# Reordering the pieces of a pipelined ViT block on four engines

## The reference, cut to what matters

```python
h = layernorm(layernorm(patches(x)) @ W + b)         # 768 -> 192 (tok)
h = h + attn(ln(h))        # 12 heads of 16, causal, with a relative term, then a projection
n = ln(ln(h))              # the routed block
s = sigmoid(n @ Wr + br);  idx = top_k(-s, 29)       # 29 of 196 tokens
attn_out = softmax(q k / 4) v @ Wo + bo              # kept for the 29 tokens only
mix_out  = (n + s * pooled) @ Wm + bm                # for all the others
h3 = h + where(selected, attn_out, mix_out)
out = h3 + gelu(ln(h3) @ W1 + b1) @ W2 + b2          # 192 -> 768 -> 192
```

## Time and profile before

| what | value |
|---|---|
| median of 3 runs | 4944.79 us |
| the profiled execution's own time | 4944.02 us |
| its span in the profile | 4942.2 us |
| TensorE busy, matmuls | 4696.2 us (95%) |
| VectorE busy | 3872.3 us (78%) |
| ScalarE busy | 3448.9 us (70%) |
| GpSimd busy | 3065.9 us (62%) |
| granted TensorE clock, mean | 0.989 of full |

### The profile page before, as it was taken

One profiled execution on the slowest core, in us unless ns is written; L12 is line 12 of the kernel. 1 busy time (PEld: TensorE's weight loads), 2 busy tenths in 40 slices (PEclk: granted clock), 3 DMA queues, 4 the chain that ended last, 5 costly groups with the idle time before them and its releaser, 6 DMA issues. The chain is left out here.

```text
span 4942.2 us, 143405 instructions
## 1 busy us (share of the span) xinstructions
PE 4696.2 (95%) x44376; PEld 4299.3 (87%) x44376; DVE 3872.3 (78%) x13015; ACT 3448.9 (70%) x12030; POOL 3065.9 (62%) x4143
## 2 busy tenths in 40 slices
PE   3899999999999999999999999999999999999998
PEld 3788888888888888888888888888888888888887
DVE  3787887887888788788788878878878877887885
ACT  1667777776776777777677677777777767767775
POOL 2566666666666666666666666666666666666664
PEclk7899999999999999999999999999999999999999
DMA  5555555455555555555555555555554555555551
GB/s 70 68 68 72 69 71 72 66 74 67 69 73 67 72 70 70 72 67 73 69 67 74 67 70 72 68 72 69 71 71 66 74 67 69 72 67 72 70 70 21
DMA packets 339085, 340.16 MB, mean 69 GB/s; under 512 B 47652, under 2 KB 306033, under 8 KB 339057
## 3 DMA queue, kind: packets, MB, share of 16 engines
q1 hardware_dynamic: 332522, 337.37, 52.3%
q10 hardware_dynamic: 6535, 2.45, 0.3%
HBM read 204.78 MB, written 19.27 MB: 45 GB/s over the span
## 5 line engine op out<-in xcount | busy, mean ns | idle before, releaser
L1610 ACT ACTIVATE p<-banks,negmax 98x98 f32<-98x98 f32 (+1 forms) x3072 | 1139.3, 379 | 216.9 <-issue 121.8
L544 POOL TENSOR_TENSOR p<-p,rden 98x392 f32<-98x392 f32 x1152 | 980.9, 870 | 280.8 <-DVE rden L1242 280.7
L1226 DVE TENSOR_REDUCE negmax<-banks 98x2 f32<-98x392 f32 (+1 forms) x1152 | 609.6, 557 | 141.0 <-PE banks L732 122.2
L732 PE MATMUL banks<-kz,qparts 128*98 128x392 f32 x2304 | 648.9, 385 | 0.0
L1610 ACT ACTIVATION_READ_ACCUMULATOR p<-banks,negmax 98x1 f32 x3072 | 612.0, 199 | 0.0
L743 PE MATMUL banks<-tokw,x_sb 128*98 128x193 f32 x3072 | 592.4, 336 | 15.5 <-POOLq L556 14.6
L743 PEld LDWEIGHTS banks<-tokw,x_sb 128*98 128x98 f32 x3072 | 553.9, 252 | 20.3 <-issue 14.6
L767 PE MATMUL banks<-ident,p 98*98 98x98 f32 x4608 | 530.4, 252 | 24.1 <-ACTq L1614 4.1
L695 PE MATMUL banks<-z3Ts,w_split 128*128 128x196 f32 x3840 | 508.4, 279 | 33.7 <-ACT gT L1685 32.3
L695 PEld LDWEIGHTS banks<-z3Ts,w_split 128*128 128x128 f32 x3840 | 468.2, 192 | 64.2 <-ACT gT L1685 58.0
L535 POOL TENSOR_TENSOR gparts<-gT,gparts 128x392 fp32r<-128x392 f32 x384 | 395.2, 1040 | 190.9 <-DVE gparts L1434 190.9
(11 more groups left out here) (264 smaller groups left out, 11542.3 us busy)
## 6 DMA issues: line engine op xcount, KB each, us to landing
x_sb<-in_x SPq DMA_DIRECT2D x384, 196.0 KB, 5.0
kz<-kq SPq DMA_DIRECT2D x1024, 73.5 KB, 2.6
x_sb<-in_x SPq DMA_DIRECT2D x256, 190.8 KB, 8.9
x_sb<-in_x SPq DMA_DIRECT2D x256, 185.5 KB, 11.1
qparts<-kq SPq DMA_DIRECT2D x256, 147.0 KB, 2.7
x_sb<-in_x SPq DMA_DIRECT2D x128, 189.0 KB, 7.3
out<-out_row SPq DMA_DIRECT2D x128, 147.0 KB
pT<-in_L_ffn_W ACTq DMA_DIRECT2D x1, 576.0 KB
```

Source lines behind the costliest of these rows:

```text
L544: gp.tensor_tensor(heads, heads, rden[:, g, t, s0:s0 + sn].unsqueeze(2).broadcast_to([HT, sn, w]), ALU.mult).then_inc(sem["pnorm_sb"], 1)
L732: last = mm(o, qparts[:, g, HT * t:HT * t + HT], kz[:, slots[0]:slots[-1] + 1, part, g, 0:w], start=False, stop=part == 1, skip_group_chec ...
L1226: ve.tensor_reduce(negmax[:, g, t, slots[0]:slots[-1] + 1], bank[RING[f"S{k}"]][0:HT, 0:w * len(slots)].rearrange("p (s w) -> p s w", w=w) ...
L1610: sc.activation((p1 if t else p0)[0:HT, 4 * g + s], bank[b][0:HT, w * i:w * i + w], ACT.Exp, bias=negmax[:, g, t, s:s + 1], accum_out=den[ ...
```

## The change

Nothing is added to or taken from any list: the same pieces with the same waits stand in other orders on TensorE, VectorE, ScalarE and GpSimd. SyncE's list, which issues the transfers, is as it was. The orders that the prediction speaks of, as the diff has them:

```diff
 # GpSimd
-                if back:
-                    gp.drain()
-                    gp.tensor_tensor(h2b[:], h2[:], both(bf2), ALU.add).then_inc(sem["h2b_sb"], 1)
                 if front:
                     normalised(0)
...
+                if front:
+                    normalised(6)
                 if back:
                     gp.wait_ge(sem["rden2_sb"], after("rden2_sb", m))
...
+                if front:
+                    normalised(7)
                 if head:
                     gp.wait_ge(sem["y_stat"], after("y_stat", l))
                     rstd(mv_y[:, :, 1], ve2[:], rstd2[:], "y_rstd")
                 if front:
-                    normalised(6)
-                if front:
-                    normalised(7)
-                if front:
                     normalised(8)
+                if back:
+                    gp.drain()
+                    gp.tensor_tensor(h2b[:], h2[:], both(bf2), ALU.add).then_inc(sem["h2b_sb"], 1)
+                if tail:
+                    gelu_low(0)
```

More of the change, by code:

```diff
@@ L619, in step @@
                         sem["f_rstd"], 1)
+                if back:
+                    gp.wait_ge(sem["h3_stat"], after("h3_stat", m))
+                    rstd(mv_3[:, :, 1], ve5[:], rstd5[:], "h3_rstd")
                 if back:
@@ L992, in step @@
                 if back:
+                    score()
                     keys2()
-                    score()
                 if head:
@@ L1002, in step @@
                     causal("S1")
+                if back:
+                    gather()
+                if front:
                     causal("S2")
@@ L1049, in step @@
                     causal("B2")
+                if back:
+                    attn_out()
                 if tail:
                     up(2)
-                if back:
-                    attn_out()
+                if front:
+                    attention()
                 if head:
                     attention_cols()
-                if front:
-                    attention()
                 if back:
@@ L1468, in step @@
                     maxima(1)
+                if back:
+                    sigmoid()
+                    kept_rows()
+                if front:
                     maxima(2)
[L1470 to L1473, removed]
                 if back:
-                    kept_rows()
+                    mix()
                 if front:
@@ L1478, in step @@
                     inverse_sums(1)
[L1479 to L1482, removed]
+                    maxima(3)
                     maxima(4)
                     maxima(5)
-                    inverse_sums(3)
                     maxima(6)
@@ L1488, in step @@
                     q_blocks()
+                if front:
+                    inverse_sums(2)
+                    inverse_sums(3)
                 if head:
@@ L1493, in step @@
                     maxima(7)
+                if tail:
+                    mlp_cols_lo()
+                if front:
+                    inverse_sums(5)
                 if back:
@@ L1496, in step @@
                 if front:
-                    inverse_sums(5)
+                    transposed("A0")
+                    maxima(8)
+                    inverse_sums(6)
+                if back:
+                    inverse2()
                 if head:
                     embedding()
-                if back:
-                    inverse2()
                 if front:
-                    maxima(8)
-                    inverse_sums(6)
-                    transposed("A0")
+                    inverse_sums(7)
                 if head:
@@ L1514, in step @@
                 if front:
+                    inverse_sums(8)
                     transposed("A3")
+                if back:
+                    context2()
+                if tail:
+                    gelu_parts(0)
                 if head:
@@ L1518, in step @@
                 if back:
-                    context2()
+                    attn_out()
                 if head:
@@ L1522, in step @@
                 if tail:
-                    gelu_parts(0)
                     gelu_parts(1)
-                if back:
-                    attn_out()
+                if front:
+                    attention()
+                if tail:
+                    gelu_parts(2)
                 if head:
                     attention_cols_lo()
-                if tail:
-                    gelu_parts(2)
-                if front:
-                    attention()
-                if back:
-                    merge()
                 if front:
@@ L1537, in step @@
                 if back:
-                    mlp_input()
+                    merge()
                 if head:
@@ L1542, in step @@
                     routed_input()
+                if back:
+                    mlp_input()
                 if tail:
@@ L1692, in step @@
                     values()
+                if back:
+                    keys2()
+                if head:
+                    squares()
+                if front:
                     load_table(ACT.Exp)
                 if back:
-                    keys2()
                     exp_scores()
-                if head:
-                    squares()
                 if tail:
@@ L1704, in step @@
                     softmax(0)
-                    softmax(1)
                 if back:
@@ L1708, in step @@
                 if front:
+                    softmax(1)
                     softmax(2)
-                    softmax(3)
                 if back:
@@ L1713, in step @@
                 if front:
+                    softmax(3)
                     softmax(4)
```

32 lines of the change are left out of this document (9 added, 23 removed).

## The result

The changed kernel took 5121.58 us (median of three runs, 5119.95 to 5124.74), against 4944.79 us before: a ratio of 1.0356, 95% interval 1.0333 to 1.038. The forecast was 4988 us with a range of 4900 to 5050: the direction was right, the size four times too small. The profiled execution has a span of 5119.7 us, 177.5 us more than before.

A forecast was written before the change was run, and what follows sets the result against it. TensorE was taken as the bound, in 125 steps of 37.40 us. Longer and shorter waits cancelled at 37.40; collisions added 0.35, giving 37.75 us per step, +44 us in all: 4988 us, 8-in-10 range 4900 to 5050.

The forecast's parts named there:

- Failed step 1: VectorE's chain ahead of `up(1)`: `max2` done at 18.4 us into the step, 18.2 before, so ScalarE's `softmax2` starts at 18.5.
- Term 3: VectorE's `embedding_scaled` collides with GpSimd's `normalised(7)` at SBUF, delaying `embedding_normalised`: 0.35 us per step, bounds 0 and 0.8.
- Rival (b): Behind `up(1)`: `embedding_normalised` done by t = 24.2, so 0.45 of 0.66 us of waits go; 4894 us, chance 0.19.
- Rival (c): ScalarE reaches `softmax2` 0.4 us later, behind `mix`, and the collision costs 0.8: +1.1 us per step, 5080 us, chance 0.09.

## Why the prediction was right and wrong

Places in a step of the full clock (medians, in us from the transposes that start it; the last two columns are lengths; the forecast adds 0.07 for the next step's first pieces):

| | `mlp_cols_lo` late | multiplication of L1253 held | `softmax2` starts | `embedding` done | TensorE reaches `up(1)` | `up(1)` starts | to the end | step |
|---|---|---|---|---|---|---|---|---|
| forecast | yes | no | 18.5 | 20.75 | 19.27 | 20.75 | 16.93 | 37.75 |
| changed kernel | yes | yes | 19.06 | 21.24 | 19.69 | 21.39 | 16.84 | 38.23 |
| `inverse_sums(2)`, `(3)` late | yes | no | 18.69 | 20.88 | 19.33 | 21.03 | 17.52 | 38.55 |
| `mlp_cols_lo` early | no | yes | 18.29 | 20.48 | 19.29 | 20.62 | 16.84 | 37.47 |
| `mlp_cols_lo` early, `inverse_sums(3)` late | no | no | 18.21 | 20.40 | 19.29 | 20.55 | 17.22 | 37.77 |

Right in kind: TensorE waits once a step at `up(1)` for `embedding`, the waits before L875 and L939 are gone, A5 waits for L544, L1282 ran free (mean 0.410 us instead of 0.701) and so did `wkeep` (0.221 instead of 0.514, forecast near 0.17).

Right in number by luck: the wait itself (1.70 us, forecast 1.5, bounds 1.2 to 1.9; 192 us marked in all, forecast 190). `embedding` was 0.49 us late against the forecast, and TensorE reached `up(1)` 0.42 us late, since the late `mlp_cols_lo` also holds up `up(0)`, which the prediction left out; with it early TensorE arrives at 19.29, as forecast. From `up(1)` to the end 16.84 us came and 16.93 were forecast, but 0.35 of these were a collision that cost nothing; waits behind `up(1)` took 0.92 us, forecast without the collision 0.66 (before A5 0.4 for 0.30, between `projection` and `down` 0.3 for 0.10).

Failed step 1, the largest single error in the step: "I get it done at 18.4 (18.2 before), so `softmax2` starts at 18.5". `max2` was done at 19.02 and `softmax2` started at 19.06. `patch_variance`'s multiplication, 0.162 us on the mean before, took 0.631, since the new order of VectorE's reciprocals released `normalised(3)` just ahead of it. Term 3 had named this mechanism and looked for it in two places, and not at the two-number instructions between them. The table has what it did: without the hold `softmax2` starts at 18.69, so 0.37 of the 0.56 us are the hold's and 0.19 an underestimate of `mlp_cols_lo`. The two don't simply add: moving `mlp_cols_lo` is worth 0.77 us at `softmax2` with the hold and 0.48 without, and the hold is worth 0.08 once `mlp_cols_lo` is early, when ScalarE is the limit. That a late `softmax2` is on the path is shown by the run that moved `mlp_cols_lo` (0.76 us a step). No run shows the hold's own price in the step: both runs that removed it delayed GpSimd's products and lost more behind `up(1)`. A smaller miss of the same sum: it let `up(1)` start the moment `embedding` is done; in these runs 0.14 to 0.15 us lie between them.

Failed step 2: term 3 put 0.35 us on the collision at `embedding_scaled`. The collision came, with 0.30 us more on the mean of each of two instructions, and cost nothing (5122.88 against 5121.58 us), because VectorE had to wait for A2 behind it. `up(1)` started 0.64 us later than forecast, and the 0.35 us that were forecast and not needed hid part of that: the short step was forecast as 37.75 and came as 38.23.

Failed step 3, the largest by its absence: the clock. The prediction read "at the full clock" from the earlier trace rows and never asked what a standstill of 1.5 us would do to it. That is 74 us of the 133 us by which the forecast was short (5122 less 4988); the other part is the 0.48 us of the step, 60 us.

Rival (b), faster, had its condition (`embedding_normalised` done by t = 24.2) missed: it ended at 25.3. Rival (c) had named late ScalarE through `mix`; ScalarE was late through `max2` instead.

What stays open: why TensorE's or GpSimd's old list in the changed kernel costs 1130 and 290 us more was read from waits only, and no run took these apart. Exchanging VectorE's or ScalarE's list alone in the changed kernel wasn't tried. Nor is it known why the clock fell behind one standstill of 1.70 us and not behind the next.

## What to carry to other kernels

When a wait of the bound engine is added, follow the releaser's chain back with each instruction's length as it will be beside its new neighbours, down to the smallest ones; 0.16 us can become 0.63. Then look for a piece that fits into an idle time of that chain: here one piece moved ahead of three others was worth 0.76 us a step and the clock besides. And a longer standstill of TensorE can have a second price behind it, the clock, which useless work in the gap averted here (5121.58 to 5047.21 us).

## What the runs showed of the hardware

The length of the standstill did not decide it alone. The same 1.70 us brought the clock down in 44 of 119 steps of the changed kernel and left it up in 75; with GpSimd's old list, in steps of 40.9 us, 14 of 122 steps had the half clock. The Trainium skill ("TensorE: Matmul & The Clock Gate", "Why this matters for your kernels") sets its rule for gaps between bursts of matmuls at longer ones than these; the measurement decides.

A multiplication of two numbers per row (L1253) went from 0.16 to 0.64 us when it started 0.22 us into a GpSimd product of 0.84 us, and ended with it. A VectorE instruction that reads one tensor in SBUF and a scalar per row was held as well: `sel` (L1314, 98 x 32, a compare), of which there are two in a step. In the changed kernel the second took 1.2 us instead of 0.24, ending with the first of GpSimd's sums of squares (L561), which had started 0.04 us ahead of it; the mean of the two went from 0.240 to 0.708 us. VectorE stood idle for 0.75 us soon behind it. The Trainium skill ("SBUF — State Buffer", "Who interferes with whom") lists such an operation among those that can take both ports and so contend with GpSimd; the trace agrees.
